# GpSimd waits for each chunk's gathers to land before it issues the next chunk's: a four-layer graph network on one core

## The reference

```python
h = relu(layernorm(x)); x = x + L0(h)   # sum of h[src] * weight over edges, divided by degree, two 64x64 products
h = relu(layernorm(x)); x = x + L1(h)   # attention: softmax over each node's edges of w1[dst] - w2[src] + d(edge),
                                        # then the sum of a * (w3[src] + d); d is a small MLP of 3 edge attributes
h = relu(layernorm(x)); x = x + L2(h)   # MLP with batch norm over edges of [h[src], edge_attr], mean, MLP over nodes
h = relu(layernorm(x)); x = x + L3(h)   # sum of h[src] over edges
```

## Time and profile before

| | |
|---|---|
| median of 3 runs | 2036.69 us (2029.17 to 2037.15) |
| profiled execution, span from the first instruction to the last | 2601.9 us |
| TensorE busy | 1601.6 us, 62% of that span |
| VectorE busy | 1551.6 us, 60% |
| GpSimd busy | 1327.9 us, 51% |
| ScalarE busy | 895.7 us, 34% |
| TensorE clock granted, mean | 0.747 of full speed |

### The profile page before, as it was taken

The page is one execution under the profiler, slowest core; times in us unless marked ns, Lnnn a source line. Parts: engine busy times, 40 slices in busy tenths (PEclk is TensorE's granted clock), DMA queues, the critical chain, the costliest instruction groups (busy, mean ns, idle before and its releaser), DMA issues.

```text
span 2601.9 us, 23168 instructions
## 1 busy us (share of the span) xinstructions
PE 1601.6 (62%) x6953; PEld 1209.1 (46%) x6953; DVE 1551.6 (60%) x2430; ACT 895.7 (34%) x1175; POOL 1327.9 (51%) x1397
## 2 busy tenths in 40 slices
PE   1546554555565655555665247888786725889892
PEld 1334433443354444444453235666565514767672
DVE  5445545554477477677776635554555934868783
ACT  1222222222231755555553113332333811433340
POOL 6555555455534455555664455446551036656554
PEclk8566666666676777787787568898897657989896
DMA  6111211121121344444444313323224602333332
GB/s 141 36 51 54 63 52 51 53 63 52 52 68 54 99 142 145 139 141 147 145 146 129 83 37 70 69 59 75 65 65 101 204 13 53 85 78 84 78 79 57
DMA packets 223807, 219.66 MB, mean 84 GB/s; under 512 B 108066, under 2 KB 170967, under 8 KB 223447
## 3 DMA queue, kind: packets, MB, share of 16 engines
q1 hardware_dynamic: 175575, 147.75, 19.3%
q0 software_dynamic: 44384, 56.98, 10.5%
q10 hardware_dynamic: 3744, 13.63, 1.3%
HBM read 116.77 MB, written 101.46 MB: 84 GB/s over the span
## 4 chain that ended last, share of the span: by engine, by line
PE 23%; another core or an unknown queue 13%; issue 11%; DVE 11%; ACT 5%; POOL 3%; DMA 2%; SPq 1%; DVEq 0%; POOLq 0%; ACTq 0%
PE psum L993 16%; POOL arena L676 3%; PE psum L1018 1%; DVE scan_ring L1935 1%; DVE spare L1935 1%; DMA maxima<-arena 1%; DVE arena L1810 1%; PE psum L1085 1%; ACT spare L1257 1%; DVE arena L1816 1%; PE psum L1024 1%; ACT spare L1331 1%; DMA keep<-keep_rows 1%; DVE spare L1760 1%
## 5 line engine op out<-in xcount | busy, mean ns | idle before, releaser
L636 POOL DMA_INDIRECT gathered<-table,idx x1264 | 1208.6, 956 | 1014.9 <-issue 363.6
L1760 DVE COPY_PREDICATED spare<-spare,psum 64x512 f32<-64x512 uint8 x300 | 220.8, 736 | 303.7 <-ACT spare L1355 208.2
L993 PE MATMUL psum<-rounded 128*128 128x512 f32 x1144 | 303.8, 419 | 63.8 <-issue 43.4
L993 PEld LDWEIGHTS psum<-rounded 128*128 128x128 f32 x1144 | 227.3, 202 | 124.9 <-issue 59.2
L780 PE MATMUL psum<-ident,arena 128*128 128x128 f32 x416 | 107.9, 409 | 287.5 <-ACT arena L1140 272.1
L1592 DVE TENSOR_REDUCE rs<-arena 128x16 f32<-128x1024 f32 x52 | 63.4, 1219 | 302.3 <-ACT arena L1144 249.6
L780 PEld LDWEIGHTS psum<-ident,arena 128*128 128x128 f32 x416 | 69.8, 205 | 354.9 <-ACT arena L1140 284.0
L1144 ACT ACTIVATE arena<-psum 128x1024 f32<-128x1024 f32 x52 | 53.3, 1025 | 410.9 <-remote 280.3
L1355 ACT ACTIVATE spare<-psum 64x512 f32<-64x512 f32 x82 | 48.5, 592 | 397.7 <-remote 199.0
L676 POOL DMA_INDIRECT arena<-scan,rowidx x75 | 79.3, 1058 | 206.7 <-DMA scan<-ea 114.3
L906 PE MATMUL psum<-ident,arena 128*128 128x128 f32 x172 | 34.4, 335 | 189.3 <-ACT arena L1246 185.5
(11 more groups left out here) (285 smaller groups left out, 3444.9 us busy)
## 6 DMA issues: line engine op xcount, KB each, us to landing
scan<-ostage SPq DMA_DIRECT2D x130, 256.0 KB, 2.3
scan<-arena SPq DMA_DIRECT2D x52, 512.0 KB
gathered<-table,idx POOLq DMA_INDIRECT x1264
d_mlp<-arena ACTq DMA_DIRECT2D x26, 512.0 KB
arena<-d_mlp SPq DMA_DIRECT2D x52, 256.0 KB
maxima<-arena SPq DMA_DIRECT2D x52, 256.0 KB
ea<-in_edge_attr SPq DMA_DIRECT2D x104, 128.0 KB
spare<-src_row SPq DMA_DIRECT2D x100, 128.0 KB
```

The costliest lines, as they stand in the source:

```text
L636: pool.indirect_dma_start(out=out[:, j, hf, :], out_offset=None, in_=tab[layer], in_offset=bass.IndirectOffsetOnAxis(ap=idx[:, j, hf * NCH ...
L993: last = nc.tensor.matmul(P[:, bank + t, :], parts[layer][n][:, b:b + 2, :].rearrange("p b d -> p (b d)"), tile(layer, m, u)[:, hf * CH:(h ...
L1760: picked = v.copy_predicated(rows[m % 2][halves[hf], :], quarter[m % 2][halves[hf], q - 1, :], P[halves[q % 2], bank + q // 2, :])
```

## The change

A wait for the landing is put behind each chunk's eight gathers, in each of the four layers. The semaphores and the counts are those that the chunk's reader waits for; nothing else is edited.

```diff
                             gather_chunk(0, k, i, Gw(k, D, m), S("gathered", 2 * m + k))
+                            pool.wait_ge(S("gathered", 2 * m + k), n_gathered(0, n + 1))
...
                     gather_chunk(1, c % 2, c // 2, Gw(g % 2, 2 * D), S("wide gathered", g % 2))
+                    pool.wait_ge(S("wide gathered", g % 2), n_gathered(1, g // 2 + 1))
...
                 gather_chunk(2, c % 2, c // 2, Gw(g % 2, D, g // 2 % 2), S("gathered", g % 4))
+                pool.wait_ge(S("gathered", g % 4), n_gathered(2, g // 4 + 1))
...
                 gather_chunk(3, c % 2, c // 2, Gw(g % 2, D, g // 2 % 2), S("gathered", g % 4))
+                pool.wait_ge(S("gathered", g % 4), n_gathered(3, g // 4 + 1, g % 4))
```

## The result

The changed kernel takes 2346.48 us (2342.03 to 2353.49, 4 runs) where the kernel before takes 2036.47 us (2029.17 to 2037.15, 4 runs): a ratio of 1.154 [1.151, 1.157], 310 us slower. The prediction said 2129 us, with a range up to 2240.

What follows compares the result with a forecast made beforehand. It took chains between the other engines, not GpSimd's gathers, to bound the layers. In a timed run the waits would add 0, 51, 4 and 37 us in layers 0 to 3: 2037 + 92 = 2129 us, range 2033 to 2240.

Steps and rivals of the forecast that it cites:

- I let the other engines' work shrink to 0.783 in every layer: All four layers: the profiled lengths scaled by timed median over profiled span, giving 592, 448, 379 and 311 us.
- needs 582: nothing: Layer 0, timed run: it lasts 592 us and GpSimd with the waits needs 582, so no added time.
- the prediction's own needs: GpSimd's time per layer with the waits: 582, 499, 383 and 348 us for layers 0 to 3.
- The gather stays at 1.25 us in a timed run: Gathers in all layers: 0.95 us each plus 0.30 us to the next, not shrinking with the other work.
- A wait adds 1.2 us in layer 0 and 1.6 us in the others.: Behind each chunk's eight gathers: chunks take 11.2 us in layer 0, 11.6 us in layers 1 to 3, instead of 10.0.
- GpSimd already bounds the timed run: Rival, all layers: GpSimd is the bound before the change, every wait paid in full, 253 us more, 2290 us; 12%.
- The hidden cases: Rivals with shorter timed gathers: 0.98 us hides the waits, 2039 us, 22%; 1.12 us half hides them, 2052 us, 13%.
- Contention as a gain: Rival: fewer gathers in flight let other transfers and the first chunk land sooner, at most 3.8 us, 2033 us; 3%.
- 240 us in all: Changed kernel's profile: GpSimd's some 158 waits for its own landings, 1.2 us in layer 0, 1.5 to 2 elsewhere.
- The span hardly moves, while the timed median does: Changed kernel's profile: span about 2605 us against 2601.9 before, while the timed median rises to 2129 us.
- The first wait of layer 0: Layer 0 start: the load of `keep` fills the queues, so the wait holds chunk 1 for some 9 us.
- Slower, at 0.73: Whole kernel: chance 0.73 of being slower, against 0.25 for the same and 0.02 for faster.

Runs made afterwards that it cites:

- experiment 3: The kernel before, with nothing changed, profiled in the condition where it takes about 2036 us: 2023.51 us, span 2021.8 us.
- experiment 1: The kernel before unchanged, profiled again: ratio 1.001, span 2600.6 us; with the wait in layer 0, 1, 3 or 2 alone: 0.956, 0.991, 0.991, 0.975.

## Why the prediction was wrong, step by step

**The profile was taken for a longer picture of the timed run. Wrong, and this was the step that failed.** "I let the other engines' work shrink to 0.783 in every layer" gave layers of 592, 448, 379 and 311 us. They are 523, 459, 338 and 314 (experiment 3). The two profiles of the kernel before differ by 580 us, and little of that is stretched work: VectorE, ScalarE and GpSimd are as busy in one as in the other to within 6 us, and TensorE is busy 109 us longer. The rest is idle time; layer 0 alone is 234 us longer, and there the other engines were held. The worst number is layer 0, "needs 582: nothing". With the prediction's own needs and the true lengths the sum is 59 + 40 + 45 + 34 = 178 us and 2215 us, in place of +92 and 2129. The sign that was overlooked was on the page: 13% of the chain with no owner. And "no row tells which stretches are shorter when nothing is recorded" looked for the cause in the recorder; experiment 1 excludes that.

**The gather stays at 1.25 us in a timed run. Right**: 0.944 us at median and 0.30 us between two in the 2036 us condition too.

**"A wait adds 1.2 us in layer 0 and 1.6 us in the others." Too small**: by the windows 111.5 / 52 = 2.1 us, then 2.1, 2.0 and 1.8 us. The landing was read well in quiet (1.1 us, 1.2 predicted). The wake-up was taken from a wait for VectorE, 0.26 us; after a landing it is 0.65 us (408.2 to 408.85). In layer 0 the first gather after a stop is longer by 0.45 us at most chunks, which was not in the sum. In layer 1 the gap grows by 2.5 us at median, where the sum had 1.6. This term is worth the other 131 us of the miss of 217.

**The rivals.** "GpSimd already bounds the timed run", 12%, is what happened, with its mechanism: every wait paid in full. Its 2290 us is low by the size of the term: 158 x 2.0 = 316 us gives 2353. The argument against it ("all four layers at once would have to be so") was an argument from the wrong profile. The hidden cases need a shorter gather, which isn't there. Contention as a gain was rated 3%; a gain exists, worth 10%, but in the other condition, and it needs no wait for a landing: memsets do it too. Full queues are not what it relieves either, as far as the one window shows: the DMA share is 0.12 while the engines are held.

**What the profile would show.** 158 waits for landings: right (152 in one row of the table). 240 us in all: 360. The waits for readers shrink: all but 8.9 us vanish. "The span hardly moves, while the timed median does": the span fell by 262 us, since the two profiles are of different conditions. The readers starve in layers 1 and 3: in all four, and in layer 0 VectorE waited for gathers 48 times (116 us) without the change already. The first wait of layer 0, some 9 us: right (10.3).

**Slower, at 0.73: right**, but by costs in layers 1 and 3 that make up 92 of the 310 us; that layer 0 pays most (111.5 us) was in no case but the 12% one.

## What to carry to other kernels

Before a profile is used, hold its span against the median of the timed runs. Here they differed by a quarter because the profile was of another condition, and a share of the chain without an owner (13%) was the sign of it; scaling such a profile evenly hides which engine is the bound. A wait for a DMA's landing directly behind its issue costs an issuing engine that is the bound about 2 us each time, and the same wait four issues later costs nothing. Take the price of a wake-up from a wait of the same kind (a landing, not an engine), and look whether the first instruction behind it is longer too: here it was in one layer of four.

## What the runs showed of the hardware that was not expected

- One and the same program takes 2030 or 2600 to 2665 us; at 2600 us, stretches are found in which VectorE and ScalarE stand still (11 us in the one shown) while GpSimd issues gathers back to back.
- A pause of 2.0 us on GpSimd after every eight gathers takes 11% off in that condition, and one of 0.74 us takes 1%.
- In layer 0 the first gather after a wait for a landing takes 1.39 us in place of 0.94 us at most chunks; in the other layers it doesn't, and after a memset gap of 1.38 us it takes 0.95 us in every layer.
- At the chunk read, GpSimd starts again 0.65 us after the last packet of a landing, and VectorE 0.5 us after it.
- A memset of 0.12 us between two gathers moves their spacing only from 1.250 to 1.258 us.
